# The last layer's bilinear sums with one operand in the accumulator

## The reference

```python
x_off = g_lt[:, None] * gather(q_lt_x, q_lt_y) + g_rb[:, None] * gather(q_rb_x, q_rb_y) \
      + g_lb[:, None] * gather(q_lt_x, q_rb_y) + g_rt[:, None] * gather(q_rb_x, q_lt_y)
x_off = x_off * mm                      # modulation per position
return conv2d(x_off, w_conv, None, ks, 0)   # 3x3 taps, stride 3
```

## Time and profile before

| | us |
|---|---|
| median of 3 runs | 14167.45 |
| lowest, highest | 14162.11, 14221.47 |
| the profiled execution, device time | 14118.1 |
| its span | 14115.9 |

### The profile page before, as it was taken

One profiled execution on the slowest core, in us unless ns is written; L12 is line 12 of the kernel. 1 busy time (PEld: TensorE's weight loads), 2 busy tenths in 40 slices (PEclk: granted clock), 3 DMA queues, 4 the chain that ended last, 5 costly groups with the idle time before them and its releaser, 6 DMA issues. The chain is left out here.

```text
span 14115.9 us, 114139 instructions
## 1 busy us (share of the span) xinstructions
PE 7635.1 (54%) x29878; PEld 2752.4 (19%) x29878; DVE 6134.4 (43%) x8183; ACT 4795.1 (34%) x7391; POOL 7386.6 (52%) x7857
## 2 busy tenths in 40 slices
PE   7666676666666666666329997233233333333322
PEld 2222222222222222222112332111111111111111
DVE  2334334343343333533445665445444454544544
ACT  6544454444444444444115664111011111111100
POOL 0354554545545365464750000667676777777776
PEclk9888787788878878887559998555556555565655
DMA  0222222222222222222663334524243343433332
GB/s 8 66 76 77 81 80 79 73 78 78 77 75 75 73 84 75 78 83 81 165 162 80 83 81 91 128 92 117 92 115 106 106 118 99 116 98 101 100 95 87
DMA packets 1169070, 1280.20 MB, mean 91 GB/s; under 512 B 795966, under 2 KB 924414, under 8 KB 1164670
## 3 DMA queue, kind: packets, MB, share of 16 engines
q0 software_dynamic: 338688, 925.30, 21.6%
q1 hardware_dynamic: 815710, 347.84, 10.4%
q10 hardware_dynamic: 14368, 3.21, 0.1%
HBM read 1080.00 MB, written 195.82 MB: 90 GB/s over the span
## 5 line engine op out<-in xcount | busy, mean ns | idle before, releaser
L420 POOL DMA_INDIRECT b_gathered<-table,b_iu x3528 | 3558.4, 1009 | 2419.5 <-DVE b_sample L895 1192.4
L420 POOL DMA_INDIRECT d_gathered<-table,d_iu x3528 | 3716.0, 1053 | 1499.1 <-issue 1066.7
L516 PE MATMUL PS<-b_key 64*128 64x448 f32 (+1 forms) x5600 | 1602.8, 652 | 1213.0 <-ACT b_weights L690 909.0
L538 PE MATMUL PS<-ident,d_sample 128*128 128x128 f32 (+1 forms) x1960 | 513.3, 427 | 2815.0 <-DVE d_sample L895 1707.1
L690 ACT ACTIVATE b_weights<-PS 128x896 f32<-128x896 f32 (+1 forms) x1400 | 1273.0, 909 | 1791.5 <-remote 1189.3
L526 PE MATMUL PS<-b_weights,b_values 128*64 128x448 f32 (+1 forms) x5600 | 1545.8, 635 | 270.0 <-issue 156.2
L883 DVE TENSOR_TENSOR d_gathered<-d_gathered,PS 128x2304 f32<-128x2304 f32 x392 | 1000.7, 2553 | 857.6 <-DMA d_gathered<-table,d_iu 788.1
L693 ACT ACTIVATE b_weights<-b_weights 128x896 f32<-128x896 f32 (+1 forms) x1400 | 1332.7, 952 | 44.7
L699 ACT ACTIVATE d_sampleT<-PS 128x512 f32<-128x512 f32 x392 | 233.7, 596 | 2713.2 <-PE PS L538 1444.5
L883 DVE TENSOR_TENSOR b_gathered<-b_gathered,PS 128x2304 f32<-128x2304 f32 x392 | 999.6, 2550 | 112.7 <-DMA b_gathered<-table,b_iu 100.8
L918 DVE TENSOR_TENSOR b_x<-b_x_att,PS 128x448 f32 x56 | 34.8, 622 | 2109.2 <-PE PS L526 1623.3
(11 more groups left out here) (224 smaller groups left out, 9944.8 us busy)
## 6 DMA issues: line engine op xcount, KB each, us to landing
b_gathered<-table,b_iu POOLq DMA_INDIRECT x3528
d_gathered<-table,d_iu POOLq DMA_INDIRECT x3528
l_x_and_h<-xs SPq DMA_DIRECT2D x224, 224.0 KB, 3.9
hs<-l_hT SPq DMA_DIRECT2D x224, 224.0 KB, 2.8
d_h<-hs SPq DMA_DIRECT2D x32, 1554.0 KB
table<-b_table_rows SPq DMA_DIRECT2D x208, 128.0 KB, 1.9
table<-d_table_rows SPq DMA_DIRECT2D x208, 128.0 KB
xs<-b_key SPq DMA_DIRECT2D x14, 1568.0 KB
```

What stands on the lines that cost most here:

```text
L420: pool.indirect_dma_start(GB[:, g, k, :], None, tables[b], bass.IndirectOffsetOnAxis(ap=ix, axis=0)).then_inc(gathered[g], 16)
L516: mm = pe.matmul(PS[0:keys(k), 2 * (k % S_BUFS) + a, 0:CH], KEY[r, 0, k * P:k * P + keys(k)], KEY[r, 0, j * CH:(j + 1) * CH], start=True, ...
L538: mm = pe.transpose(PS[0:n, 5 + 2 * (s // 4), (s % 4) * P:(s % 4 + 1) * P], S[:, t % 2, s * P:s * P + n], K.ident[:, :])
```

## The change

In the last layer alone, the three steps of a tile become five. `RIGHT`, 9 taps by 128 floats in PSUM banks 2 to 4, takes the weighed right corners; the left corners are weighed in place. The column sums are two: right corners of row 1 into `RIGHT`, those of row 0 in place in `GB`. The row sum reads `GB` and `RIGHT`. Each VectorE instruction of the five has one tensor operand in SBUF and one in PSUM. Since there is one `RIGHT`, the weighing of a tile now also waits for the row sum of the tile before. The layer `b_` keeps its code.

```diff
+        RIGHT = None if att else PS[:, 2:5, :].rearrange("p b f -> p (b f)")[:, 0:TAPS * P].rearrange("p (k f) -> p k f", f=P)
...
+            def weigh_apart(c, t):
+
+                g = t % G_BUFS
+                v.wait_ge(gathered[g], (c * USES[g] + t // G_BUFS + 1) * 16 * TAPS)
+                v.wait_ge(samples_ready, c * TPC + t + TPC)
+                g4 = GB[:, g].rearrange("p k (q c) -> p k q c", q=4)
+                w4 = W4[:, t * TAPS:(t + 1) * TAPS, :].unsqueeze(3).to_broadcast([P, TAPS, 4, C])
+                right = RIGHT.rearrange("p k (q c) -> p k q c", q=2)
+                v.tensor_tensor(right, g4[:, :, 2:4, :], w4[:, :, 2:4, :], ALU.mult).then_inc(weighed, 1)
+                v.tensor_tensor(g4[:, :, 0:2, :], g4[:, :, 0:2, :], w4[:, :, 0:2, :], ALU.mult).then_inc(weighed, 1)
+
+            def add_columns_apart(c, t):
+                gx = GB[:, t % G_BUFS]
+                v.wait_ge(weighed, (c * TPC + t) * 4 + 3)
+                v.tensor_tensor(RIGHT[:, :, C:P], gx[:, :, C:P], RIGHT[:, :, C:P], ALU.add).then_inc(weighed, 1)
+                v.tensor_tensor(gx[:, :, 0:C], gx[:, :, 0:C], RIGHT[:, :, 0:C], ALU.add).then_inc(weighed, 1)
+
+            def add_rows_apart(c, t):
+                gx = GB[:, t % G_BUFS]
+                v.wait_ge(weighed, (c * TPC + t) * 4 + 5)
+
+                v.wait_ge(samplesT_mm, c * TPC + t + (1 if t else 2))
+                v.tensor_tensor(S[:, t % 2].rearrange("p (k c) -> p k c", c=C), gx[:, :, 0:C], RIGHT[:, :, C:P], ALU.add)\
+                    .then_inc(samples_ready, 1)
...
-                                weigh_corners(c, t)
+                                weigh_corners(c, t) if att else weigh_apart(c, t)
                             elif k % 3 == 1:
-                                add_columns(c, t)
+                                add_columns(c, t) if att else add_columns_apart(c, t)
                             else:
-                                add_rows(c, t)
+                                add_rows(c, t) if att else add_rows_apart(c, t)
```

## The result

| | before | after |
|---|---|---|
| median, us | 14175.9 (4 runs, 14162.11 to 14221.47) | 14479.67 (4 runs, 14465.6 to 14553.26) |
| the profiled execution, us | 14118.1 | 14470.36 |
| last layer in it (first to last gather) | 5260 | 5629 |

After / before is 1.0204, with a 95% interval of 1.0172 to 1.0237: the changed kernel is slower by 2.0%. The forecast was 14,450.

The account below looks back on a forecast made before the run. GpSimd's row of gathers was taken to bound the last layer. Chunks of 97.7 us x 56 = 5471, plus 73 for loads and VectorE, gave 5544 against 5260: +284 us, predicting 14,450, range 13,920 to 14,700.

Parts of the forecast that it names:

- Part 1: Last layer's column and row sums, reading one operand in PSUM, block no gather: -298 us of GpSimd time, net some -220.
- The 65 us kept for the loads of a pair: Stretching expected to stay in the last layer: 2 x 7 gathers of 5.59 instead of 0.95 us.
- Part 2: VectorE's work for a last-layer tile grows 0.3 us, 4.7 to 5.0; mostly hidden, costing 8 us in all.
- the bound of half speed: VectorE instructions reading and writing PSUM might run at half speed: +1.2 and +0.6 us a tile, 55 us uncovered.
- Part 3: The wait for the row sum delays only VectorE's next weighing; already in the 0.3 us a tile, other engines unmoved.
- Part 4: Without stretched gathers as rests, each last-layer chunk ends starved: GpSimd waits 14 us a chunk (bounds 11 and 19); chance 0.56.
- The signs: Last-layer checks: gathers about 965 ns, over 50 waits and some 750 us, L939 10 to 25 us after the convolution.
- gaps of 1.1 us between the position steps: Sign: VectorE's small steps for the next positions would wait 1.1 us in place of 0.03 as the rule.
- the second wait: Late position steps make GpSimd wait again in the same chunk: 10 us in every third chunk, up to 20.8.
- The gain is kept: Rival, chance 0.29: slow signals only coincide with unbroken gathers, so -220 + 8 = -212 us, 13,955.
- Rests move: Rival, chance 0.12: GpSimd takes its some 10 us of rest a chunk as one wait, not seven stretches; 14,170.
- The stretches stay: Rival, chance 0.03: VectorE's work as such holds gathers, so the PSUM operands gain nothing and 8 us are lost; 14,175.

Follow-up runs that it names:

- the second group: Follow-up runs on another chip than the result's; there the unchanged kernel before took 13,709 us and the unchanged changed kernel 14,091 us, ratio 1.0295.
- e1_rest1: Changed kernel plus one GpSimd memset of 128x1000 ahead of the fifth gather of each last-layer tile: 13,597 us, 0.9987 of the kernel before.

## Why the prediction was right

**Part 1, the gathers.** Forecast -298 us of stretching, measured -349. The 65 us kept for the loads of a pair mostly went too: 14 gathers of 5.6 us were expected to stay, but GpSimd now often stands waiting while they run, and six over 3 us are left. By the Trainium skill ("SBUF — State Buffer", "Who interferes with whom") a VectorE instruction with at most one SBUF input does not contend with GpSimd; the trace agrees (954 ns). Its probe, in which tensor_tensor did not stall a GpSimd-issued DMA, is not what this kernel shows: 1049 against 970 ns between two kernels that both had rests and no waits.

**Part 2, VectorE.** 1362 and 1347 ns for the weighings, 761 and 747 for the column sums: a read and a write in PSUM cost no more than the formula, and the bound of half speed is out. From one weighing to the next are 4.99 us (the chunk above: L921 of the first tile ends 11286.3), as forecast.

**Part 3, the new wait.** 2.4 us of idle time of L907 end on L921 in the whole layer.

**Part 4, the rests, the term that decides.** The mechanism was the one stated: GpSimd stops after its fourth tile, L939 follows 5.0 us after its last gather (4.6 in the sum), the wait is 12.19 us (11 in the sum). The term taken at 14 us a chunk measured 937.4 / 56 = 16.7. Its two parts were both mis-sized: the first wait is 12.2, not 11 (the four pieces that the prediction names, 4.6, 1.4, 5.1 and 0.8, add up to 11.9); the second was taken as 10 us in every third chunk and is some 4.6 us in nearly all. A third part was named but not priced: at the start of a pair the wait was 38 us in four of eight pairs. Of the +153 us that this gives above the sum's 784, the larger gain of part 1 took 51 back and smaller items 17: +284 forecast, +369 measured in the layer between the profiled executions. The rest of the program took 17 us less. The profiled execution of before lay 58 us under its median and that of after 9 under, so the medians differ by 304 only. That the total came within 30 us is thus partly luck: the layer alone was 85 us off, of which the spread between executions took 49 back and the rest of the program 17. It was also forecast for this chip without knowing that chips differ; on that of the second group the same change led to 14,091 us.

**The signs.** Gathers 954 ns (965 forecast), waits 100 and 937 us (over 50, some 750), L939 10 to 25 us after the convolution in 37 of 56 chunks and a little more in 15: as said. One failed: gaps of 1.1 us between the position steps did not become the rule. There are 68 of 0.9 to 1.25 us among 1792 steps of the changed kernel, about one a chunk, against 123 before. Gaps of half that size took their place, though (270 of 0.3 to 0.9 us, against 128), so both kinds together cost about the same, 205 and 196 us. In the chunk above the steps come 5 to 25 us after a wait of GpSimd, which I read as its rest. The sum had no term for these gaps beyond the second wait.

**The rivals.** "The gain is kept" fell with the 54 of 55 slow chunks, and its premise with `e1_rest1`: the late finishes don't merely fall together with unbroken gathers, they vanish when GpSimd's row is broken up. "Rests move" was nearest in kind: GpSimd did trade seven stretches for waits, but at 16.7 us for 10; that a wait costs more because it comes only after 46 us without a rest is my reading, and no run shows it by itself. "The stretches stay" fell with the 954 ns.

## What to carry to other kernels

Where one engine issues indirect gathers in an unbroken row, the other engines can go on tens of microseconds late; in the profile it is idle time that ends on `remote` or on an instruction long done, growing with the length of the row. A stall removed from such a row may have been its rest: put a short instruction of another kind in its place (here some 1 us in 12 on GpSimd) before judging the change. In the last layer that turned a loss of 2 to 3% into nothing or a gain of 0.5% (0.9987 with one rest of 0.95 us, 0.9949 with two of 0.535 on another chip). The 3.7% and 7.2% came when the first layer got rests too, and lie mostly there. Ask of each stage what it waits for before giving it rests: they pay where the waits are long (858 us and more in the first layer), and cost where they are short (72 us in the last layer of the kernel before).

## What the runs showed of the hardware

- 372 us of GpSimd memsets added to each of two layers made the kernel before 2.8% faster (first layer 583 us shorter, last layer 219 longer); with the changed sums it was 3.7% on one chip and 7.2% on another.
- The sum of the rests per tile counts (2 x 0.535 us as good as 0.95 on one chip; 0.70 there and 0.535 on another not enough; 0.95 leaves no wait over 1.1 us on two chips, and 25 waits on a third). I read this as a backlog that the gathers build up faster than it drains; which queue or port holds it stays open. Whether it takes a pause or only fewer gathers per microsecond was not separated either. A kernel with fewer completion signals per gather would tell more; it wasn't tried.
- It doesn't depend on bytes: half the data in each gather, the same 98.5 us a chunk.
- Chips differ in it: the medians of the same kernel before are 13,624 to 14,252 us. In the two traces of it the durations of VectorE's and GpSimd's instructions are the same (a gather's mean is 1053 and 1058 ns), and the waits are not (196 against 72 us in the last layer, 1192 against 942 in the first).
- VectorE with both an input and the output in PSUM runs at the pace of an output in SBUF: 1362 against 1347 ns for 1152 elements, where two SBUF operands took 1358.
